# Graph attention with routed FFN on one core: output projection in split half precision, turned by a DMA, one task per tile in the shared PSUM bank

## What is computed

```python
x = x + attention(layernorm(x), adj)         # 8 heads of 16, masked softmax
#   q, k, v = x@Wq+bq, x@Wk+bk, x@Wv+bv ; scores = q k^T / 4, masked by adj
#   out = softmax(scores) @ v ; out @ Wo + bo
x = x + ffn(layernorm(x))                     # shared expert + top 2 of 8 routed experts
#   shared = gelu(x@W1s+b1s)@W2s+b2s ; routed = sum_e mask_e * (gelu(x@W1p_e+b1p_e)@W2p_e+b2p_e)
```

## Time and profile before

| | |
|---|---|
| median of three runs | 1326.36 us |
| the profiled execution: its time, its span | 1322.85 us, 1321.0 us |
| busy over the span: PE, DVE, ACT, POOL | 83%, 75%, 66%, 65% |
| busy in 300 to 400 us (attention, mid loop): PE, DVE, ACT, POOL | 95.7, 84.0, 83.2, 78.3 of 100 us |
| granted TensorE clock in that stretch | 1.00 |

### The profile page before, as it was taken

How to read it: one execution, slowest core, us unless ns; L and a number is a source line. 1 busy time by engine, 2 the same in 40 slices (tenths; PEclk the granted TensorE clock), 3 DMA queues, 4 the chain that set the end, 5 groups by cost and what they waited for, 6 DMA issues and landing times. The chain is left out here.

```text
span 1321.0 us, 39795 instructions
## 1 busy us (share of the span) xinstructions
PE 1093.3 (83%) x12580; PEld 785.2 (59%) x12581; DVE 995.3 (75%) x2407; ACT 866.2 (66%) x1705; POOL 853.4 (65%) x897
## 2 busy tenths in 40 slices
PE   0789999999999999994389999799999999989100
PEld 0456666666666666663167677577777777768100
DVE  3468888888888888885486888587777777767398
ACT  0577788888888888882277788567666666568000
POOL 3125677777778777776676677277777777766300
PEclk9999999999999999998699999999999999999755
DMA  2112333333333333222345554344444444334399
GB/s 76 29 47 71 86 90 91 94 92 94 94 96 93 81 88 93 74 60 69 95 121 143 140 158 116 65 94 100 101 101 93 98 96 96 79 67 80 114 355 306
DMA packets 276549, 136.54 MB, mean 103 GB/s; under 512 B 195142, under 2 KB 254700, under 8 KB 276474
## 3 DMA queue, kind: packets, MB, share of 16 engines
q1 hardware_dynamic: 242938, 93.39, 29.3%
q0 software_dynamic: 16896, 33.86, 8.2%
q10 hardware_dynamic: 16640, 8.39, 2.1%
HBM read 47.95 MB, written 54.04 MB: 77 GB/s over the span
## 5 line engine op out<-in xcount | busy, mean ns | idle before, releaser
L1377 POOL DMA_INDIRECT pairs_dram<-x_rows x272 | 279.1, 1026 | 123.4 <-issue 80.8
L1055 ACT ACTIVATE hid<-Z,biases 128x512 f32<-128x512 f32 (+1 forms) x336 | 207.9, 631 | 139.9 <-PE Z L1023 86.2
L1070 DVE SCALAR_TENSOR_TENSOR h<-hid,h 128x512 f16<-128x512 f32 (+1 forms) x288 | 183.5, 650 | 53.6 <-ACT h L1046 49.2
L474 DVE TENSOR_REDUCE smin<-S 128x8 f32<-128x1024 f32 x128 | 155.8, 1217 | 88.9 <-PE S L740 87.4
L1035 PE MATMUL Y<-w,h 128*128 (+1 forms) x3168 | 193.6, 221 | 11.6 <-DVE h L1070 8.7
L1035 PEld LDWEIGHTS Y<-w,h 128*128 128x128 f16 x3168 | 186.2, 99 | 28.4 <-issue 11.9
L1168 POOL DMA_INDIRECT slots_dram<-x_rows,pair_slot x128 | 132.4, 1034 | 48.2 <-issue 23.0
L1023 PE MATMUL Z<-x_rows,w 128*128 128x512 f16 (+1 forms) x720 | 147.5, 351 | 11.5 <-DMA x_rows<-slots_dram 5.9
L335 POOL DMA_INDIRECT slots_dram<-x_rows,pair_slot x116 | 118.7, 1023 | 29.1 <-issue 16.6
L477 DVE TENSOR_TENSOR probs<-smin,S 128x768 f32<-128x768 f32 x128 | 122.1, 954 | 14.4
L1046 ACT ACTIVATE h<-hid 128x512 f16<-128x512 f32 (+1 forms) x176 | 105.8, 601 | 21.0 <-ACT hid L1055 5.6
(11 more groups left out here) (212 smaller groups left out, 2192.0 us busy)
## 6 DMA issues: line engine op xcount, KB each, us to landing
y_pairs<-pairs_dram SPq DMA_DIRECT2D x32, 512.0 KB, 6.1
x_res<-in_x_dram SPq DMA_DIRECT2D x32, 256.0 KB, 3.3
adj<-in_adj_dram SPq DMA_DIRECT2D x32, 256.0 KB
xT_dram<-xT SPq DMA_DIRECT2D x32, 256.0 KB, 3.4
xTu<-xT_dram SPq DMA_DIRECT2D x32, 256.0 KB
out_dram<-x_res ACTq DMA_DIRECT2D x16, 512.0 KB, 10.7
pairs_dram<-x_rows POOLq DMA_INDIRECT x272
slots_dram<-x_rows,pair_slot POOLq DMA_INDIRECT x256, 2.5
```

Source lines behind the costliest of these rows:

```text
L474: dve.tensor_reduce(smin[:].rearrange("p (r e) -> p r e", e=2), S_heads, AX_X, ALU.min).then_inc(s["min_done"], 1)
L1055: act.activation(self.hid[:, c, 0:w], self.bank(b, c)[:, 0:w], ACT.Gelu, bias=bias[:, c:c + 1], scale=1.0 / (XS * WS)).then_inc(self.gelu_ ...
L1070: dve.scalar_tensor_tensor(out=self.piece(b)[:, 1, c, 0:w], in0=self.hid[:, c, 0:w], scalar=HS, in1=self.piece(b)[:, 0, c, 0:w], op0=ALU.m ...
L1377: pool.indirect_dma_start(pairs_dram, bass.IndirectOffsetOnAxis(ap=pair_of[n][:, j:j + 1], axis=0), y_sb[n % NY][:, j], None, bounds_check ...
```

## The change

1. The attention output is kept in one buffer rather than two, with a factor `XS` in it (V is no longer divided by it), and split: ACT writes the high halves (`high_output`, at the end of slot 2), DVE the low halves (`low_output`, slot 3).
2. PE no longer turns it: SP issues one DMA transpose of 256 KB (`turn_output`). The last group alone is still turned by PE, and split on its way out of PSUM.
3. The output product is 12 f16 products of 128 columns, in place of four f32 ones.
4. `turn_normed` is one DMA transpose of 256 KB in place of four of 64 KB.
5. Each slot of PE has one task of the bank M0 behind the products with V: `out`, Q, K, V in slots 0 to 3; `lg` stands ahead of the first half of PT in slot 0. ACT's copies move with them.
6. On DVE the second layer norm's statistics go from slot 3 to slot 2, and `mask` from slot 2 to slot 3.
7. On POOL `norm1` stands behind the first scatter, and the other three scatters ahead of `low_half` and `split`. On ACT `high_half` goes ahead of the second copy of PT in slot 3.

```diff
-    M0_ORDER = [("aT", 2, "aT_sb"), ("out", 2, "x2_done"), 
-                ("Q", -1, "q_sb"), ("K", -1, "k_sb"), ("V", -1, "v_sb"), ("lg", 3, "lg_sb")]
+    M0_ORDER = [("lg", 4, "lg_sb"), ("out", 2, "x2_done"),
+                ("Q", -1, "q_sb"), ("K", -1, "k_sb"), ("V", -1, "v_sb")]
...
# SP
-            for j in range(GT):
-                sp.dma_start_transpose(xnT[:, g % 2, :, j * P:(j + 1) * P], xn16[:, j].rearrange("p a c -> p (a c)"))\
-                    .then_inc(s["xnT_in"], 16)
+            sp.dma_start_transpose(xnT[:, g % 2].rearrange("p j a t -> p (j a) t"),
+                                   xn16[:, :, :, :].rearrange("p j a c -> p (j a c)")).then_inc(s["xnT_in"], 16)
+        def turn_output(g):
+            wait(sp, "asplit_done", g + 1)
+            wait(sp, "out_ps", g)
+            sp.dma_start_transpose(aT16[:, :, :, :].rearrange("p j a t -> p (j a) t"),
+                                   at16[:, :, :, :].rearrange("p j a c -> p (j a c)")).then_inc(s["aT_in"], 16)
...
             store_xT(g - 6)
+            if g - 4 < NG - 1:
+                turn_output(g - 4)
             if g - 1 < NG:
                 turn_normed(g - 1)
...
# POOL
             if late:
                 scatter(g - 5, 0, g * GT)
-            if late:
-                scatter(g - 5, 1, g * GT + 1)
             if has(g, -2):
                 norm1(g + 2, g % 2)
             if late:
+                scatter(g - 5, 1, g * GT + 1)
                 scatter(g - 5, 2)
+                scatter(g - 5, 3)
...
-            if late:
-                scatter(g - 5, 3)
...
# DVE
+        def low_output(g):
+            wait(dve, "ahi_done", g + 1)
+            dve.tensor_tensor(at16[:, :, 1], attn[:, :, :, :].rearrange("p j h c -> p j (h c)"), at16[:, :, 0],
+                              ALU.subtract).then_inc(s["asplit_done"], 1)
...
+                if j == 3 and has(g, 1):
+                    low_output(g - 1)
                 if j == 3 and has(g, 4):
                     place(g - 4, q)
...
-                if j == 2 and has(g, -1):
-                    mask(g + 1, 1 - q)
-                if j == 3 and has(g, 2):
+                if j == 2 and has(g, 2):
                     stats2(g - 2)
                     gather2(g - 2)
+                if j == 3 and has(g, -1):
+                    mask(g + 1, 1 - q)
...
# PE
             elif task == "out":
...
+                    wait(pe, "aT_in", (g + 1) * 16)
...
-                    mm = pe.matmul(bank[:, j * P:(j + 1) * P], attnT[:, j * P:(j + 1) * P], wo[:], start=False, stop=j == GT - 1)
+                    for n, (k, m) in halves():
+                        mm = pe.matmul(bank[:, j * P:(j + 1) * P], aT16[:, j, m], wo16[:, k],
+                                       start=False, stop=j == GT - 1 and n == 2)
...
-                tasks = {0: (None, ("aT", g - 2, q), None), 1: (None, ("out", g - 2, q), None),
-                         2: (("Q", g + 1, 1 - q), ("K", g + 1, 1 - q), None),
-                         3: (None, ("V", g + 1, 1 - q), ("lg", g - 3, 1 - q))}[j]
+                tasks = {0: (("lg", g - 4, q), None, ("out", g - 2, q)), 1: (None, None, ("Q", g + 1, 1 - q)),
+                         2: (None, None, ("K", g + 1, 1 - q)), 3: (None, None, ("V", g + 1, 1 - q))}[j]
```

More of the change, by code:

```diff
@@ L91, in attention_phase @@
     oT = sb("oT", [P, 2, P])
[L92 to L96, removed]
+    attn = sb("attn", [P, GT, H, HD])
+    at16 = sb("at16", [P, GT, 2, P], F16)
+    aT16 = sb("aT16", [P, GT, 2, P], F16)
+    wo16 = sb("wo16", [P, 2, P], F16)
+    wq, wk, wv, bias_rest = (attn[:, n].rearrange("p h c -> p (h c)") for n in range(GT))
+    bo_rows, bv_mat, out_bias, ones = (at16[:, n].rearrange("p a c -> p (a c)").bitcast(F32) for n in range(GT))
+    before = aT16[:, 0].rearrange("p a c -> p (a c)").bitcast(F32)
     xc2 = xn
@@ L433, in residual @@
             xg = x_res[:, bass.ds(g * GT, GT), :]
-            dve.tensor_tensor(xg, bank[:, :].rearrange("p (j c) -> p j c", j=GT), xg, ALU.add).then_inc(s["x2_done"], 1)
+            dve.scalar_tensor_tensor(out=xg, in0=bank[:, :].rearrange("p (j c) -> p j c", j=GT), scalar=1.0 / (XS * WS),
+                                     in1=xg, op0=ALU.mult, op1=ALU.add).then_inc(s["x2_done"], 1)
+        def low_output(g):
+            wait(dve, "ahi_done", g + 1)
+            dve.tensor_tensor(at16[:, :, 1], attn[:, :, :, :].rearrange("p j h c -> p j (h c)"), at16[:, :, 0],
+                              ALU.subtract).then_inc(s["asplit_done"], 1)
         def stats2(g):
@@ L551, in drain @@
             choose(a - 2, 0)
+            wait(dve, "ahi_done", NG)
+            dve.tensor_tensor(aT16[:, :, 1], last_aT, aT16[:, :, 0], ALU.subtract).then_inc(s["asplit_done"], 1)
             residual(b, LAST[b, "out"])
@@ L568, in high_half, with high_output @@
             wait(act, "xn_ready", g + 1)
-            wait(act, "xnT_in", g * GT * 16)
+            wait(act, "xnT_in", g * 16)
             act.activation(xn16[:, :, 0], xn[:], ACT.Copy).then_inc(s["xhi_done"], 1)
+        def high_output(g):
+            wait(act, "norm_done", (g + 1) * GT // 2)
+            wait(act, "aT_in", g * 16)
+            act.activation(at16[:, :, 0], attn[:, :, :, :].rearrange("p j h c -> p j (h c)"), ACT.Copy)\
+                .then_inc(s["ahi_done"], 1)
         def evac(task, g, q):
@@ L584, in evac @@
                                M0[:, :].rearrange("p (j c) -> p j c", c=HD), ACT.Copy,
[L585 to L588, removed]
+                               scale=1.0 / WS).then_inc(s["v_sb"], 1)
             elif task == "lg":
@@ L621, in step @@
                     evac(*a)
+                if j == 3 and has(g, -2) and not (isinstance(g, int) and g < 0):
+                    high_half(g + 2)
                 if has(t, 1, NT):
@@ L630, in step @@
                     act.activation(oT[:], OD[:, 0:2 * P].rearrange("p (a t) -> p a t", a=2), ACT.Copy).then_inc(s["o_sb"], 1)
-                if j == 3 and has(g, -2) and not (isinstance(g, int) and g < 0):
-                    high_half(g + 2)
+                if j == 2 and has(g, 1):
+                    high_output(g - 1)
         def drain():
@@ L641, in drain @@
                 act.activation(oT[:], OD[:, 0:2 * P].rearrange("p (a t) -> p a t", a=2), ACT.Copy).then_inc(s["o_sb"], 1)
-            evac("aT", NG - 1, 1)
+            act.wait_ge(last_aT_ps, 1)
+            wait(act, "out_ps", NG - 1)
+            act.activation(aT16[:, :, 0], last_aT, ACT.Copy).then_inc(s["ahi_done"], 1)
             for g in range(NG - 3, NG):
@@ L663, in m0_task @@
                 if task == "Q":
-                    wait(pe, "xnT_in", (g + 1) * GT * 16)
+                    wait(pe, "xnT_in", (g + 1) * 16)
                 m0_free(pe, task, step_g)
@@ L678, in m0_task @@
                 wait(pe, "norm_done", (g + 1) * GT // 2)
-                bank = last_bank(g, task)
-                if bank is not M0:
-                    wait(pe, "sub_done", NT)
-                    wait(pe, "direct_done", NT)
-                else:
-                    m0_free(pe, task, step_g)
+                wait(pe, "sub_done", NT)
+                wait(pe, "direct_done", NT)
                 for j in range(GT):
-                    mm = pe.transpose(bank[:, j * P:(j + 1) * P], attn[:, q, j].rearrange("p h c -> p (h c)"), ident[:])
-                mm.then_inc(s["aT_ps"], 1)
+                    mm = pe.transpose(last_aT[:, j], attn[:, j].rearrange("p h c -> p (h c)"), ident[:])
+                mm.then_inc(last_aT_ps, 1)
             elif task == "out":
-                wait(pe, "aT_sb", g + 1)
                 bank = last_bank(g, task)
@@ L692, in m0_task @@
                     m0_free(pe, task, step_g)
+                else:
+                    wait(pe, "sub_done", NT)
+                    wait(pe, "direct_done", NT)
+                if isinstance(g, int) and g == NG - 1:
+                    wait(pe, "asplit_done", NG)
+                else:
+                    wait(pe, "aT_in", (g + 1) * 16)
                 pe.matmul(bank[:, :].rearrange("p (j c) -> p j c", j=GT), sel[:],
```

35 lines of the change are left out of this document (19 added, 16 removed).

## The result

The changed kernel takes 1472.86 us (median of 4 runs, 1467.88 to 1474.77), beside 1326.55 us for the kernel before on the same chip: 1.110 times as long, 95% interval 1.107 to 1.113. That is inside the range, on the forecast side, and 44 us above the 1429 forecast. Most of the difference is in one of the four tile slots: slot 3 is 1.34 us a step longer than forecast, 39 us in all, slot 1 adds 12, and slot 0 takes 8 back.

What follows compares the result with a forecast made beforehand. PE's queue was taken as the bound: a step grows from 17.38 to 20.90 us, 29 x 3.52 = +102; with step 31 +3, startup -4 and last group +1, 1425 profiled, 1429 median, range 1355 to 1487 (8 in 10).

Steps and rivals of the forecast that it cites:

- The bound: Attention loop: PE, busy 96%, decides; tasks moved from the gap to slot ends lengthen the step, 18.57 us without DMA waits.
- The wait of `out`: Slot 0: the output product waits 2.33 us for the turned output, landing taken as 4.0; the slot lasts 7.19 us.
- Q behind the residual: Slot 1: Q waits for DVE's residual addition behind the subtraction, idling PE about 0.6 us; the slot lasts 4.94 us.
- Slot 3: Loop's last tile slot: plain tile 3.56, ranks 0.31 and V's task 0.69, together 4.56 us.
- the 20 to 22 that were to show the forecast: Sign in the profile after: a loop step of 20 to 22 us, with 20.90 forecast.
- Edits priced at nothing: ACT's copies, POOL's order, and DVE's statistics and mask moves were taken as covered by slack, at no cost.
- rival C: Loop: the DMA wait also drops PE's clock, 1.5 us in every step, 44 us on top: 1473 us; chance 0.15.
- Rival B: Slot 0: the turned output is there in time, so a step takes 18.57 us, the kernel 1359; chance 0.18.
- Startup: Before the loop: one earlier transpose removes a 1.81 us wait and most of its half clock, -4 us (0 to -6).
- From the execution to the median: Whole kernel: the median of the runs was put 3.5 us above the profiled execution, 1429 for 1425.

Runs made afterwards that it cites:

- e7: e10 with PE's tasks moved back to their old places, mostly in the gap ahead of PT's second half, and V's copy with them: 1304.10 us.
- e10: Changed kernel with mask in slot 2, statistics in slot 3, `place` ahead of `low_output`, and `high_half` behind the second copy of PT: 1395.64 us.
- e1: Changed kernel with SP's turning of the output put ahead of the adjacency load, the x load and the store: 1408.30 us.
- e8: Changed kernel with ACT's `high_half` put back behind the second copy of PT in slot 3: 1451.07 us.
- b2: Kernel before with GpSimd's new order and ACT's `high_half` ahead of the second copy of PT, nothing else: 1344.20 us.
- e5: Changed kernel with DVE's mask back in slot 2 and the second layer norm's statistics back in slot 3: 1402.83 us.
- b1: Kernel before with one DMA transpose of 256 KB for the normalised rows in place of four of 64 KB: 1311.18 us.
- b3: Kernel before with GpSimd's new order alone, `high_half` staying where it was: 1322.76 us.
- e2: Changed kernel with DVE's `place` put ahead of `low_output` in slot 3: 1496.58 us.

## Why the prediction was right, and what it missed

- **The bound.** Right: PE's queue was the bound, and what decides is where it waits. Tasks ahead of the next scores cost what the gap used to hide; e7 against e10 prices that at 3.0 us a step. What the gap hides differs: e7's product of 0.88 us lengthens it by 0.25, but in the earlier trace rows V's 0.69 us lengthens it by 0.52, which the prediction called little.
- **The wait of `out`.** Right in kind and size: e1 takes 61 us away where the prediction had 2.33 x 29 = 68. e1's figure holds 13 us of clock. The wait is 1.68 us on average, not 2.33. Slot 0 came out at 6.93 for 7.19 by three errors that offset, and that it is close is luck. The turning goes out 1.06 us after slot 0's scores, not 2.28, because slot 3 is longer; the landing was taken as 4.0 us and has a mean of 4.72; from the bias product to the scores it is 1.15, not 0.91.
- **Q behind the residual.** Right: 0.74 of wait for `x_res` in slot 1 (e10, e1 and after alike), slot 1 at 5.08 for 4.94 where the clock is full.
- **Slot 3, the term that was mis-sized.** 4.56 was forecast, 5.90 measured: 1.34 x 29 = 39 us. It takes the step, 22.50, past the 20 to 22 that were to show the forecast. In the step shown (5.86): scores to PT 1.22 for 1.40, PT to PT 1.63 for 1.29 (K's copy on ACT), PT to the products with V 1.60 for 0.59 (`place` behind `low_output`), these to V 0.58, V to scores 0.83 for 0.69. The third is the large one, +1.01. I had `low_output` and `place` in DVE's chain towards SP, and did not ask who else waits for `place`. My own sums would have told it: `place` cannot begin before the subtraction ends, 3.61 after the scores, and PE comes to the products 1.40 + 1.29 + 0.59 = 3.28 after them. With `low_output` between, the products would start at 3.61 + 0.68 + 0.18 = 4.47 (measured 4.45, 409.43 to 413.88) and slot 3 would last 4.47 + 0.59 + 0.69 = 5.75.
- **Edits priced at nothing.** Wrong. The mask beside `low_half` costs 0.45 in the step's longest chain (e8, which undoes it, takes 22 us off in all, clock included). K's copy was said to be covered by the start of slot 3; it is not (PT to PT above). GpSimd's order with the earlier `high_half` costs 20 us in the kernel before (b2), though no instruction of the two edits is longer by itself.
- **The clock (rival C).** Half right. Where it falls for the whole stretch, as in the step shown, it costs 0.94 in slot 1 and 0.83 in slot 0 (bias product to scores 1.82; 0.99 in e1, 404.62 to 405.61), near C's 1.5. But it falls in 10 of the 29 steps, and on average costs 0.45 us a step, 13 us in place of C's 44. That C's sum, 1473, is the measured time is chance: most of what the forecast missed is in slot 3.
- **Rival B**, the output there in time: e1 and e5 make it so, and take 1408 and 1403, not 1359. Most of the gap to B's sum is slot 3 again (e1: 6.01 for 4.56).
- **Startup.** -4 forecast, -3.9 measured, and the wait of 1.81 us with its half clock is gone, as forecast. The transpose alone gives 5.7 (b1); the changed kernel gives some of that back, its scores of step 2 starting after an idle 0.73.
- **From the execution to the median.** The forecast put the median 3.5 above the profiled execution; it is 0.9 below. Without that error the 44 us would be 49.

## What to carry to other kernels

A task moved out of a gap in which its engine waits costs its whole length, and whatever its own inputs make it wait. For each moved instruction on a helper engine, list every engine that waits for it and for what now stands behind it, not only the one on the chain you follow. And when one engine's order changes, look at which of DVE's and GpSimd's instructions then run side by side: b2 and b3 differ by one copy on ACT, 1.5 us earlier in the step, and by 20 us.

## What the runs showed of the hardware

VectorE and GpSimd hold each other up instruction by instruction. A DVE instruction of 32 numbers per partition that takes 0.19 us alone took 0.70 and 1.08 and ended 0.05 us behind GpSimd's, begun before it (b2: 488.27 to 488.22, 489.45 to 489.40); `low_output` took 1.60 for 0.69 (e2); the mask 0.87 for 0.42. Not all do: the row minimum of S, from PSUM, has a mean of 1.21 to 1.23 in every run, and beside GpSimd's L293, 1.04 us on 4 numbers per partition, `logits` took its 0.19 (b3). GpSimd's `low_half`, begun second in after, took 1.31 for 1.16.

The Trainium skill ("SBUF — State Buffer", section "SBUF: two separate sides") says that the two share one pair of ports, which whichever begins first holds for its whole instruction, if VectorE's has two inputs in SBUF and GpSimd's reads SBUF, or VectorE's runs in a mode that needs both ports; the rows of b2 and e2 agree. b3's row on L293 does not: there both read SBUF, VectorE's instruction has two inputs in it and begins second, and within POOL's span it is not held up. Here the measurement decides.

A transpose of 256 KB holds SP's queue for 1.24 us, and four of 64 KB for 5.04 (medians in e10, SP's L246 and L232): its time there goes by the transfer, about 1.25 each, not by the bytes. Behind the three loads, in the kernel after, it is more: medians of 1.45 for the output and 1.94 for the rows of Q. One in place of four took 9.6 us off the profiled span (b1). How long such a transpose takes from issue to landing, which the prediction had to guess, the page of e10 shows, where the loads go out 2 us before it (median us last):

```profile
aT<-at SPq DMA_TRANSPOSE x31, 3.0
```

By that, an estimate, some 1.7 of the 4.7 us in the kernel after go with the three transfers just ahead of it.

The lower TensorE clock comes not only behind a wait for a DMA. In e1 PE never waits for the turned output, and in 5 of the 29 steps V takes 1.46 us for 0.84, behind the waits of slot 3 (0.78 and 0.94 us in the step at 378.63).
